# Twelve squares moved from VectorE to ScalarE, and the opening steps of the hyperbolic attention placed one expert tile earlier

## What is computed

```
c     = max(-<q, k>_Lorentz, 1 + 1e-7)
d     = log(c + sqrt(c * c - 1))
score = -(d * d) / sqrt(8)
```

## Time and profile before

| | us |
|---|---|
| median of three runs | 1160.65 |
| lowest, highest | 1160.46, 1163.6 |
| the profiled execution | 1174.44 |
| its span | 1173.1 |
| PE busy in it | 942.6 |
| DVE busy | 781.1 |
| ACT busy | 584.1 |
| POOL busy | 278.3 |

### The profile page before, as it was taken

How to read it: one execution, slowest core, us unless ns; L and a number is a source line. 1 busy time by engine, 2 the same in 40 slices (tenths; PEclk the granted TensorE clock), 3 DMA queues, 4 the chain that set the end, 5 groups by cost and what they waited for, 6 DMA issues and landing times.

```text
span 1173.1 us, 21148 instructions
## 1 busy us (share of the span) xinstructions
PE 942.6 (80%) x8055; PEld 539.3 (46%) x8055; DVE 781.1 (67%) x1986; ACT 584.1 (50%) x1083; POOL 278.3 (24%) x353
## 2 busy tenths in 40 slices
PE   5687769998996375677679999998578888689999
PEld 4333324444875244455433334665123334446667
DVE  6786898852235778876678935776888786664412
ACT  2455636664745366876427783231046456234332
POOL 2842320002231647865310000001121001000000
PEclk9778979999999566887659999999569699789999
DMA  8325230012865401850124018001003000100000
GB/s 311 89 79 111 51 128 2 3 50 79 256 210 169 134 1 55 214 114 7 42 92 164 2 19 134 1 1 54 0 29 136 2 2 1 36 1 1 10 1 10
DMA packets 53609, 82.12 MB, mean 70 GB/s; under 512 B 7044, under 2 KB 35157, under 8 KB 52005
## 3 DMA queue, kind: packets, MB, share of 16 engines
q1 hardware_dynamic: 44692, 72.62, 21.8%
q10 hardware_dynamic: 7792, 6.05, 1.8%
q0 software_dynamic: 1024, 2.10, 0.6%
HBM read 59.65 MB, written 21.63 MB: 69 GB/s over the span
## 4 chain that ended last, share of the span: by engine, by line
PE 52%; DVE 29%; ACT 6%; issue 4%; POOL 4%; DMA 3%; SPq 1%; ACTq 0%; DVEq 0%; POOLq 0%
PE ps_v L812 7%; DVE mx L2198 6%; PE ps_s L1023 5%; PE ps_e L1013 5%; PE ps_e L702 4%; PE ps_e L1210 2%; PE ps_s L1197 2%; DVE mx L2190 2%; DVE ps_s L2172 2%; ACT work L1642 2%; PE ps_e L717 2%; DVE xn L2142 2%; PE ps_s L732 2%; PE ps_s L1080 1%; DMA q_stack<-mT 1%
## 5 line engine op out<-in xcount | busy, mean ns | idle before, releaser
L1642 ACT ACTIVATE work<-ps_e 128x512 f32<-128x512 f32 x406 | 223.1, 597 | 109.8 <-PE ps_e L702 105.4
L3044 POOL TENSOR_TENSOR rstd<-rstd,halves 128x2 f32<-128x2 f32 x52 | 36.8, 708 | 587.2 <-DVE rstd L2129 586.9
L2198 DVE TENSOR_REDUCE mx<-ps_s 128x2 f32<-128x1024 f32 x128 | 153.6, 1222 | 26.0 <-PE ps_s L732 23.9
L812 PE MATMUL ps_v<-work,vaug 128*32 128x256 f32 x1536 | 129.8, 413 | 4.9 <-ACT work L1630 4.9
L702 PE MATMUL ps_e<-q_stack,ctx_stack 52*128 52x256 bf16 (+1 forms) x684 | 123.2, 292 | 10.1 <-DMA q_stack<-mT 3.9
L732 PE MATMUL ps_s<-ctx_stack,q_stack 49*128 49x512 bf16 (+1 forms) x296 | 92.8, 460 | 38.3 <-DVE mx L2198 28.2
L2172 DVE CUSTOM_DVE_ANT_0 ps_s<-ps_s,work 128x512 f32<-128x512 f32 x128 | 85.6, 713 | 9.2 <-PE ps_s L771 4.1
L702 PEld LDWEIGHTS ps_e<-q_stack,ctx_stack 52*128 52x128 bf16 (+1 forms) x684 | 43.6, 97 | 81.3 <-ACT work L1642 47.7
L1745 ACT ACTIVATE work<-ps_s,keep 128x512 f32<-128x512 f32 x64 | 43.8, 687 | 68.2 <-PE ps_s L1023 66.8
L2403 DVE SCALAR_TENSOR_TENSOR x<-ps_e,gates,x 128x128 f32<-128x128 f32 x64 | 19.4, 346 | 60.9 <-PE ps_e L1013 58.0
L812 PEld LDWEIGHTS ps_v<-work,vaug 128*32 128x32 f32 x1536 | 31.6, 111 | 49.2 <-issue 36.3
(11 more groups left out here) (478 smaller groups left out, 2240.8 us busy)
## 6 DMA issues: line engine op xcount, KB each, us to landing
ffn_w<-in_L0f_up SPq DMA_DIRECT2D x30, 258.0 KB, 3.7
ffn_w<-in_L0f_down SPq DMA_DIRECT2D x30, 256.0 KB, 3.8
q_stack<-q_scr SPq DMA_DIRECT2D x32, 192.0 KB
ffn_w<-in_L1f_w SPq DMA_DIRECT2D x1, 3456.0 KB, 13.1
q_scr<-parts SPq DMA_DIRECT2D x16, 192.0 KB, 2.1
c_scr<-ffn_w SPq DMA_DIRECT2D x12, 256.0 KB, 7.4
kx_scr<-ffn_w SPq DMA_DIRECT2D x12, 256.0 KB, 4.0
ctx_stack<-kx_scr SPq DMA_DIRECT2D x2, 1536.0 KB
```

What stands on the lines that cost most here:

```text
L812: m = pe.matmul(ps_v[j * COLS:(j + 1) * COLS, 0:S], values(b * nkt + k, g % 4 * GROUP + j), pt[:, j % 2, k % 2, :], start=(k == 0), stop=( ...
L1642: act.activation(pt[:, parity, :, :].rearrange("p k q -> p (k q)"), bank[exp_bank(use, h, parity)], ACT.Exp).then_inc(exped, 1)
L2198: m = dve.tensor_reduce(mx[:, b, :, pair, part], ps_s[i][:], AX, ALU.max, negate=True)
```

## The change

`EARLY_AT` is moved up by one tile for every step. The squares of DVE, their semaphore and their table go away; ACT makes them in `l1_sqrt`, each directly in front of its root and followed by a wait of ACT for its own result (`settle`). ACT waits for both clamps of the half and, for units above 0, until POOL has read `l1_s` of the unit before; DVE loses that second wait. The four squares of POOL stay.

```diff
-SQUARES = order_of([(u, n) for u in range(8) for n in range(2) if u not in POOL_SQUARES or n == 1])
...
-EARLY_AT = {3: [0], 4: [1], 5: [2], 6: [3], 8: [6], 12: [13], 13: [14]}
+EARLY_AT = {2: [0], 3: [1], 4: [2], 5: [3], 7: [6], 11: [13], 12: [14]}
...
                 if n == 0 and u in POOL_SQUARES:
                     act.wait_ge(l1_pool_sq, u - POOL_SQUARES[0] + 1)
                 else:
-                    act.wait_ge(squared, SQUARES[u, n])
+                    act.wait_ge(clamped, 4 * u + 2 * n + 2)
+                    if u > 0:
+                        act.wait_ge(added, 2 * (u - 1) + n + 1)
+                    settle(act.activation(l1_s[:, g, :], c_of(u)[:, g, :], ACT.Square))
                 act.activation(l1_s[:, g, :], l1_s[:, g, :], ACT.Sqrt, bias=minus1[:]).then_inc(rooted, 1)
...
-            if u > 0 and j % 2 and (u, n) in SQUARES:
-                dve.wait_ge(added, 2 * (u - 1) + n + 1)
             ch = c_of(u)[:, 2 * j:2 * j + 2, :]
             dve.tensor_scalar(ch, ps_s[i][:, :, 0:PACK], 1.0 + 1e-7, None, ALU.max).then_inc(clamped, 1)
-            if j % 2 == 0 or (u, n) not in SQUARES:
-                return
-            dve.wait_ge(clamped, 4 * u + j + 1)
-            c = c_of(u)[:, HALVES[n], :]
-            dve.tensor_tensor(l1_s[:, HALVES[n], :], c, c, ALU.mult).then_inc(squared, 1)
```

More of the change, by code:

```diff
@@ L450, in build @@
     qkv_ps, qkv_done = semaphore("qkv_ps"), semaphore("qkv_done")
-    near_ps, near_min, root_ps, clamped, squared, rooted, rooted_s, added, added_s, logged, far_log, least_sq = (
-        semaphore("l1_" + n) for n in ("near_ps", "near_min", "root_ps", "clamped", "squared", "rooted",
+    near_ps, near_min, root_ps, clamped, rooted, rooted_s, added, added_s, logged, far_log, least_sq = (
+        semaphore("l1_" + n) for n in ("near_ps", "near_min", "root_ps", "clamped", "rooted",
                                        "rooted_s", "added", "added_s", "logged", "far_log", "least_sq"))
```

## The result

| | before | after |
|---|---|---|
| median | 1162.40 us (1160.46 to 1163.71, five runs) | 1152.37 us (1151.08 to 1170.81, five runs) |
| the profiled execution | 1174.44 us | 1170.81 us |
| its span | 1173.1 us | 1169.5 us |

A forecast was written before the change was run, and what follows sets the result against it. The attention was taken as a ring of engines, the last to end being DVE, then POOL, then a chain through all. Terms 4.2 + 1.8 gained, less 0.2 for the opening, gave -5.8 us: median 1154.9, range 1151.5 to 1161.5.

The forecast's parts named there:

- (a): 387 to 421.5 us: DVE loses four squares, less a bank refill on PE; unit 0's exponents come 4.6 us earlier.
- (b): To 452.5 us: ACT is late at the copy of unit 0's sums, so the gain falls from 4.6 to 4.2 us.
- (c): Iteration 1: unit 3's squares stood beside waits for PE; 0.3 us for DVE, nothing for POOL's chain, not added.
- (d): Iteration 2: POOL's stretched casts shorten, ACT's logarithm limits this to 1.2; residual's wait for a square adds 0.6; total 1.8 us.
- (e): Units 3 to 7: ACT has room for 1.2 us more per iteration, DVE's squares stood beside waits; 0 gained.
- (f): Opening steps one tile earlier: tile loop ends about 0.6 us later, keys gain nothing; +0.2 us, between -0.6 and +0.6.
- ACT becomes the bound: Rival, copy of the sums in even iterations: ACT's squares delay it, +5.3 us together, 1166.2 us; chance 0.10.
- Table loads: Rival, ACT's roots: each of twelve squares brings two table loads, 30.8 us on ACT, 1175 us; chance 0.03.
- Most is given back: Rival, even iterations: ACT's 1.2 us per unit shows, POOL's 2.0 do not return; 1157.9 us; chance 0.27.
- More comes back: Rival: DVE's stretched instructions elsewhere shorten too and queries decide the opening; up to -9 us, 1151.6 us; chance 0.12.

The follow-up runs named there:

- second comparison: The whole change against the kernel before, twelve runs on another chip than the first result's: ratio 0.9961, -5.4 us with an error of 1.4.
- its fourth: The whole change against the kernel before, on a third chip: ratio 0.9950, -6.6 us with an error of 1.4.

## Why the prediction was right, and where it was wrong

**The total.** Three comparisons of the whole change on three chips gave -5.4, -5.4 and -6.6 us: -5.8 in the mean, with an error of 0.8 (-5.5 at equal clock). That is the forecast's sum, and only the first result is off it. That the two agree to a tenth is luck: single terms are off by up to 1.4 us, in both directions.

**The step that failed** is the one that turns the sum into a median: "I take the same microseconds off both", "Behind the attention nothing of the change is left, and the gain goes through to the end one to one", with "a change within 0.3% (3.5 us) can hardly be told from none here". It treats everything outside the attention as fixed. It is not: in the first pair of profiles the changed kernel is 8.2 us ahead at the exponents of unit 7 (579.19 against 570.97), and 3.6 at the end. Here is the stretch behind the attention, the same work in every kernel, as the view of windows gives it (width, busy times of PE, PEld, DVE, ACT and POOL, then the clock). The whole change in its second comparison:

```profile
588.82:1173.01 584.19, 493.95 (x3391) 266.85 (x3389) 387.52 (x934) 254.62 (x484) 47.42 (x71) 0.91 0.13 35
```

The same program in its fourth:

```profile
588.50:1180.67 592.17, 502.73 (x3391) 271.36 (x3389) 387.47 (x934) 254.89 (x484) 47.33 (x71) 0.88 0.13 34
```

The kernel before against itself:

```profile
595.96:1184.96 589.00, 501.17 (x3391) 271.26 (x3389) 387.50 (x934) 254.31 (x484) 47.33 (x71) 0.89 0.13 34
```

Of one program this stretch takes 584.2 and 592.2 us; DVE, ACT and POOL work the same to 0.3 us in both, PE 8.8 more where the clock is lower. Over all 17 profiles it runs from 583.8 to 596.6 whatever the kernel: 583.8 to 584.2 where the clock of the stretch is 0.91, 591.4 to 596.6 where it is 0.88. Over whole runs it is alike, by the 6.5 us for each 0.01 above. The first result's own five runs of the changed kernel show it: 1170.81 us at 0.872, the other four at 1151.1 to 1153.4 with 0.886 to 0.890. That is even 11 us for each 0.01; as the two pieces of the last stretch showed, it also counts where the low clock falls. By the 6.5 us, 4.2 us are 0.0065 of mean clock, by the 11 us 0.004. The one clock known of the kernel before there is 0.868, of its profiled execution at 1174.44. The clocks of the five runs of before in that result are not known, so that the missing 4.2 us are clock is likely, not shown: their cause stays open. The three later comparisons say that the change does not bring them everywhere. They cannot say that it does not on the first chip, where the whole change was compared once.

**Point by point.**

- (a) 3.2 us in place of 4.6, mis-sized: the rows above show 1.97 taken back where the sum had 0.5. This is also the prediction's own sign of being wrong ("if the exponents of unit 0 do not move by 4 us"). On the other chips, the mean of five profiles with units 0 and 1 on DVE is 38.9, of nine with ACT 35.5 us, so 3.4.
- (b) The fall from 4.6 to 4.2 did not come: 31.09 us against 31.08, forecast 31.5. The division comes 3.16 us earlier behind the first reduction (54.79 before, 51.63 now), with the exponents. That is not because ACT was early, for its copy gained 1.29 and not 2.8; PE's turn behind the copy ended 1.23 us behind the copy's end before (440.39 + 1.09 against 440.25) and 0.77 now (436.24 + 0.63 against 436.10), and DVE follows it directly, where before a stretched square stood in the way. The sum took 1.4 for that turn.
- (c) Iteration 1 kept 0.3 that the sum did not add (16.45 to 16.17).
- (d) 20.76 to 19.01 us: 1.75, forecast 1.8. The named mechanism is there: the stretched operations of POOL are gone, ACT's logarithm is next, and the turn of the maxima comes 1.33 us earlier (1.61 less the 0.28 of iteration 1) for the 1.2 of the sum; the residual no longer waits for a square, 0.6. But the two terms that the sum lacked, +0.70 on PE and -0.67 on DVE, happen to cancel, so that the total fits so well is in part luck. Here the Trainium skill's rule ("GPSIMD Engine Reference", section "1. Specifications"), which names contention on the shared SBUF interface, agrees with the rows: 1.41 and 1.23 us became 0.40 and 0.21 once the square beside them was gone.
- (e) 0.2 us in the first pair, forecast 0. The attention together: 5.4, forecast 6.0. The three later profiles of the whole change, against two with all of DVE's squares, give in means 3.2 for (a), 0.0 for (b), 0.8 for (c) and 1.1 for (d), 5.2 together, and 5.6 for the attention (187.4 against 193.0; single ones 185.9 to 188.9 and 192.6 to 193.4).
- (f) The stall, 4.33 us, was forecast at about 4.5. In the first pair the way from the start of the tiles to the first reduction is 1.3 us longer (50.78 against 49.44), where +0.2 was taken from -0.6 to +0.6; its mean clock was 0.86 against 0.91. What the term missed is the transfers: it let the keys' way cost the same after the split of the queries had moved away from it, and it became 0.8 us shorter in the first pair (4.42 to 3.58) and 0.9 on the other chips. The opening steps alone gave -1.0 with an error of 1.3, so the sign of the term is not settled; that it is worth the missing 4.2 lies outside the interval of that comparison.

**The rivals.** *ACT becomes the bound* fell: every comparison of the change is faster. Leaving ACT's squares out did not shorten the attention (187.1 us against 185.1 and 186.0 with them), and it shortened the time by 2.3 us with an error of 1.8, less than the 4 or more of a bound. The rule on mul that speaks for it (the Trainium skill, "ScalarE: Activation LUTs", "Rules for kernel authors") gives as its reason DVE's speed in bf16 with a single source; for this float32 square the traces say otherwise: 1.15 us on ACT, 1.36 at least on DVE. *Table loads* fell: none between square and root. *Most is given back*, -2.8 with cases of -2 to -3.5, lies nearly three errors or more from the mean of the three. *More comes back*, with a chance of 0.12, has the first result's size, but no stretch of the first pair shows a gain of that kind: the attention gave 5.4.

## What to carry to other kernels

A gain worked out stage by stage can come out within 1 us while the median moves by nearly twice as much: before a sum is set against a median, look at how far stretches with unchanged work move between profiles of one program, and give that its own place in the range. Work taken from a full engine does not come back whole where a neighbour stands close behind; count the waits that were hidden at each place, of PE's banks and of POOL alike. And a term that fits is to be opened all the same: two errors can cancel in it, as in iteration 2. Two transfers that follow each other closely are to be looked at together when the work ahead of one moves.

## What was not expected of the hardware

The square and the root of ACT share a table: in twelve places no load stands between them, and the attention has eight loads in front of roots and eight behind them, as before. An operation of DVE on 16 numbers, 0.17 us alone, took 1.13 us before and 1.86 now (1.13 and 1.85 on the other chips), and each time it ended with POOL's addition beside it (before 401.98 + 1.13 = 403.11 with an addition that ends at 403.07; in the changed kernel 397.38 + 1.86 = 399.24, where that addition ends at 399.21):

```profile
394.01 5.20 POOL L3098 TENSOR_TENSOR ctx_stack<-ctx_stack,work 128x1152 f32<-128x1152 f32 x2 [1.57 <-ACT work L1947]
```

So the stretching goes both ways between DVE and POOL, and a part of what DVE gains by giving up an instruction can be lost again on the next one beside POOL, here 0.73 us. And the keys' way from write to read is 0.9 us longer when it starts 0.5 us behind the queries' write than when it starts 1.45 behind, and takes 6.3 us instead of 3.4 in the one profile in which it starts just ahead of the queries' read.
